# Order of masks and scores on TensorE: rounds 3 and 4 of the row maxima as a joined pair

## The reference, cut to what matters

```
scores = einsum('bhqd,bhkd->bhqk', q, k)
rel    = einsum('bhqd,ld->bhql', q + u, pos)
scores = (scores + rel_shift(rel)) * HEAD_DIM ** -0.5
scores = where(k > q, NEG, scores)
p      = softmax(scores)
ctx    = einsum('bhqk,bhkd->bhqd', p, v)
```

## Time and profile before

| | us |
|---|---|
| median of 3 runs | 2402.88 |
| lowest and highest | 2401.92, 2403.40 |
| the profiled execution's own time | 2404.88 |
| its span, first to last instruction | 2403.1 |
| PE (TensorE matmul) busy | 2285.8 (95%) |
| PEld (weight loads, beside PE) busy | 1976.7 (82%) |
| DVE (VectorE) busy | 2023.2 (84%) |
| ACT (ScalarE) busy | 1837.5 (76%) |
| POOL (GpSimd) busy | 1146.4 (48%) |

### The profile page before, as it was taken

One profiled execution on the slowest core, in us unless ns is written; L12 is line 12 of the kernel. 1 busy time (PEld: TensorE's weight loads), 2 busy tenths in 40 slices (PEclk: granted clock), 3 DMA queues, 4 the chain that ended last, 5 costly groups with the idle time before them and its releaser, 6 DMA issues. The chain is left out here.

```text
span 2403.1 us, 83241 instructions
## 1 busy us (share of the span) xinstructions
PE 2285.8 (95%) x31360; PEld 1976.7 (82%) x31360; DVE 2023.2 (84%) x5071; ACT 1837.5 (76%) x2869; POOL 1146.4 (48%) x2089
## 2 busy tenths in 40 slices
PE   3899999999999999999999999999999999799998
PEld 3688888888888888888888888888888888677776
DVE  6789999888888888888888888888888886677774
ACT  2578888888888888888888888888878888655554
POOL 4355555554555555555454555555445553333332
PEclk8799999999999999999999999999999999899999
DMA  5543333333333333333333333333333331000000
GB/s 130 117 105 97 88 86 91 91 86 92 88 86 91 95 91 92 92 92 85 92 91 93 86 89 91 91 92 91 88 102 88 90 92 51 21 27 27 27 23 19
DMA packets 221161, 196.05 MB, mean 82 GB/s; under 512 B 28897, under 2 KB 217441, under 8 KB 220769
## 3 DMA queue, kind: packets, MB, share of 16 engines
q1 hardware_dynamic: 220768, 190.73, 29.8%
HBM read 14.46 MB, written 4.19 MB: 8 GB/s over the span
## 5 line engine op out<-in xcount | busy, mean ns | idle before, releaser
L1012 DVE TENSOR_REDUCE rowmax<-bank 128x4 f32<-128x1024 f32 (+1 forms) x768 | 914.2, 1218 | 103.3 <-PE bank L580 74.9
L817 ACT ACTIVATE probs<-bank 128x1024 f32<-128x1024 f32 x768 | 738.2, 1024 | 79.4 <-PE bank L640 78.8
L580 PE MATMUL bank<-kstack,qstack 62*128 62x256 f32 (+1 forms) x4096 | 417.9, 301 | 9.5 <-DMA qstack<-base 9.5
L640 PE MATMUL bank<-qstack,kstack 64*128 64x128 f32 (+1 forms) x4096 | 424.3, 300 | 0.0
L858 ACT ACT_TABLE_LOAD x256 | 328.4, 1283 | 4.5
L580 PEld LDWEIGHTS bank<-kstack,qstack 62*128 62x128 f32 x4096 | 317.4, 193 | 9.9 <-issue 9.9
L640 PEld LDWEIGHTS bank<-qstack,kstack 64*128 64x128 f32 x4096 | 317.1, 192 | 0.0
L602 PE MATMUL bank<-maskT_half,pick_half 64*128 64x128 bf16 (+1 forms) x3072 | 267.9, 241 | 24.5 <-DVE rowmax L1012 10.9
L542 PE MATMUL bank<-mask_half,pick_half 64*128 64x128 bf16 (+1 forms) x3072 | 268.8, 243 | 7.9 <-DVE h_all L1047 3.1
L725 PE MATMUL bank<-w,hidden 128*128 128x128 f32 x2048 | 272.6, 277 | 3.1 <-ACT hidden L867 3.1
L660 PE MATMUL bank<-probs,v_pad 128*32 128x256 f32 x4096 | 271.4, 382 | 0.6 <-DVE v_tok L993 0.6
(11 more groups left out here) (154 smaller groups left out, 5259.7 us busy)
## 6 DMA issues: line engine op xcount, KB each, us to landing
qstack<-base SPq DMA_DIRECT2D x768, 128.0 KB, 2.5
kstack<-base SPq DMA_DIRECT2D x384, 128.0 KB, 2.5
turn_x<-turn_c SPq DMA_DIRECT2D x512, 32.0 KB, 1.8
qstack<-maxrows SPq DMA_DIRECT2D x256, 16.0 KB
out<-ot SPq DMA_DIRECT2D x16, 256.0 KB, 2.4
xin<-in_x SPq DMA_DIRECT2D x14, 256.0 KB, 3.1
w<-in_w SPq DMA_DIRECT2D x4, 256.0 KB, 3.2
w_in<-in_w_in SPq DMA_DIRECT2D x1, 768.0 KB, 4.3
```

Source lines behind the costliest of these rows:

```text
L580: last = pe.matmul(bank[:, b0 + b, i * wide:(i + 1) * wide], qstack[rows, r, p0 + i, t * 128:(t + 1) * 128], kstack[rows, r, p0 + i, 0:wid ...
L640: last = pe.matmul(bank[:, b0 + b, i * wide:(i + 1) * wide], kstack[rows, r, p0 + i, kt * 128:(kt + 1) * 128], qstack[rows, r, p0 + i, q0: ...
L817: act.activation(probs[:, k], bank[:, A_BANK[k]:A_BANK[k] + 2, :], ACT.Exp, scale=SCALE).then_inc(exp_done[k], 1)
L1012: dve.tensor_reduce(rowmax[:, n % 2, t, :, p0:p0 + heads], bank[:, M_BANK[k]:M_BANK[k] + 2, :].rearrange("p b (h c) -> p b h c", h=heads), ...
```

## The change

On TensorE's list, the masks of M round 4 are moved ahead of the scores of M round 3. The wait of those masks (for exp_done[4]) moves with them. The number of instructions stays what it is, and the lists of all other engines are unchanged.

```
                 if live(s - 2):
                     m_masks(s - 2, 3)
                 if live(s - 2):
+                    m_masks(s - 2, 4)
+                if live(s - 2):
                     m_scores(s - 2, 3)
-                if live(s - 2):
-                    m_masks(s - 2, 4)
                 if live(s - 2):
                     m_scores(s - 2, 4)
                 if live(s):
```

## The result

Over 17 runs each, the changed kernel has a median of 2409.15 us (2406.41 to 2415.17) and the kernel before 2403.40 us (2400.83 to 2409.18). The forecast was +3.7 us, or 2406.6; the time lies in the range of 2401.5 to 2411.0. Two executions far off, one of e5 (4113.94 us) and one of the kernel before in the batch of e9 to e11 (6417.93 us), count in no ratio. The line of 0.2% that was to part "no change" from "slower" runs through the interval, so by that line alone the result can't be placed; that it is slower is clear.

A forecast was written before the change was run, and what follows sets the result against it. PE is busiest, but DVE's max round 1 releases f2 in each 15.33 us slot; after the change ACT's exponential gates it, 0.03 us later. Over 124 slots, 3.7 us on 2402.88 gives 2406.6, range 2401.5 to 2411.0.

The forecast's parts named there:

- line of 0.2%: Total time: a change under some 0.2%, 4.8 us or 0.039 us per slot, counts as no change, given 0.67.
- f2 is held by DVE: PE's query and key products (f2) start when DVE's max round 1 releases them; PE has about 0.12 us slack per slot.
- The join: Masks, then scores, of rounds 3 and 4 grouped on PE: 0.07 us less per slot, worth nothing alone in front of f2.
- The moved wait: Masks of round 4 on PE wait earlier for ACT's round 4 exponential and stall 0.2 us per slot.
- f2 0.02 to 0.04 later per slot: PE's query and key products load later after the stalled masks and joined scores; 0.03 us taken, over 124 slots 3.7 us.
- DVE's late round 4: DVE's max round 4 starts 0.14 us later; idle time before v_out covers it, with some 0.1 us left.
- Rival A: Round 4's masks restart slowly after the stall: 0.03 us more, 0.06 per slot, 7.4 us, 2410.3; chance 0.20.
- B: The join's gain reaches f2: each slot 0.07 us shorter, 8.7 us faster, 2394.2; chance 0.06.
- C: The stall before f2 is swallowed whole: f2 stays bound by DVE, time stays at 2402.9; chance 0.12.
- Rival D: PE drains fully before f2's load, at the score block's end: 0.10 us per slot, 12.4 us, 2415.3; chance 0.02.

The follow-up runs named there:

- e5: Changed kernel with DVE's max round 1 cut in two, f2 waiting for the first half only; 2408.29 us, ratio 1.0019 to the kernel before.
- e9: Kernel before, with the masks of round 4 placed between the two heads of the scores of round 3; ratio 1.0002.
- e11: Kernel before, with masks of round 4 between the two heads of round 3's scores and DVE's max round 1 cut in two; 2396.68 us, ratio 0.9967.
- e4: Kernel before, old order, with DVE's max round 1 cut in two and f2 waiting for the first half only; 2394.97 us, ratio 0.9970.
- e6: Changed kernel with DVE's max round 1 cut in two and ACT's round 4 exponential on half its columns; 2387.98 us, ratio 0.9939 to the kernel before.
- e7: Kernel before, old order, with DVE's max round 1 cut in two and ACT's round 4 exponential on half its columns; 2391.49 us, ratio 0.9951.
- e2: Changed kernel with ACT's round 4 exponential on half its columns from the second item on; ratio 1.0007 to the kernel before.
- e3: Kernel before, old order, with ACT's round 4 exponential on half its columns from the second item on; ratio 1.0006.
- e1: Kernel before, old order of blocks, with only the wait for exp_done[4] moved ahead of the scores of round 3; 2419.81 us, ratio 1.0075.

## Why the prediction was right

Point by point, by its own steps:

- *f2 is held by DVE, with 0.12 us of slack on PE.* Right. e4 took the hold away and the period fell by 0.11.
- *The join is worth 0.07 us and lies in front of a gate, so nothing.* Right on both counts: e6 against e7 shows the 0.07, e2 against e3 the nothing.
- *The moved wait stalls masks 4 by 0.2 us, until 0.05 or 0.06 after ACT's round 4.* Right: 0.20 us, 0.05 after it, 123 times.
- *f2 0.02 to 0.04 later per slot, 0.03 taken.* Right in size. Of the last 95 gaps between f2's starts, six in either trace are long ones (15.9 to 18.8 us); the mean of the other 89 is 15.324 before and 15.357 after, 0.033 us more. In the slots of the start, with DVE's further work, the gaps go from 15.66 and 16.07 to about 15.70 and 16.12. 124 x 0.033 = 4.1 us lies inside the measured 3.4 to 7.2. (The first ten gaps, 9.7 to 19.9 us, are no such slots; without them it is 3.9.) The forecast's 3.7 is 1.6 below the middle of the interval; whether that rest is more than spread can't be said.
- *DVE's late round 4 is covered.* Right: 0.13 us of cover are left where 0.1 was given.
- *Rival A, masks that restart slowly.* Not so: the load at 1019.32 and the first matmul of those masks start together, as in the earlier trace rows, and their loads are closer together than in flow (e1, above). The matmuls:

```profile
1019.32 0.28 PE L542 MATMUL bank<-mask_half,pick_half 64*128 64x128 bf16 x4
```

- *Rivals B and C, the gain reaches f2, or the stall is swallowed.* Not so: the period neither fell by 0.07 nor stayed; it rose by 0.033.
- *Rival D, a full drain in front of f2.* Not so. The Trainium skill (TensorEngine Tiling (Array Packing), Key Properties) says that a change of tiling mode drains the engine; here f2's first matmul starts at 1035.43, and the scores in front of it end at 1034.78 + 0.72 = 1035.50, so the measurement goes against a drain to the last modelled end.

What the prediction had right is the mechanism and its size. Its favoured outcome, a change within 0.2%, is not borne out: the interval reaches from 0.14% to 0.30%. The weak place was the line at 0.2%: a mechanism sized to 3.7 us beside a line at 4.8 us can't carry 0.67 for "no change" on its own strength, and the measured middle fell just beyond it. Of the 0.27 given to slower, 0.20 was put on rival A and 0.05 on the forecast's own spread; the latter should have had most of it.

The span of the one profiled execution rose by 2.6 us only (2403.1 to 2405.7), since one of the six long gaps was 1.5 us shorter in the trace after (17.30 against 18.78). For a change of this size the mean of the undisturbed slots tells more than two spans.

## What to carry to other kernels

Before steps are joined to save an engine time, look which semaphore opens the step behind them: time saved in front of a gate held by another engine is not seen, and a wait moved forward past work can take the gate over. Compare the due time of the moved wait with its releaser's end in one slot of the timeline; here a stall of 0.2 us stood against 0.12 us of slack and 0.07 us of gain. The gate of the step also points at the better change: cutting the releaser's instruction so that the part which is waited for comes first gave 7 to 10 us, where the join lost 5.

## What was not expected of the hardware

Cutting a reduction of 128x1024 into two of 128x512 costs DVE 0.07 us in all (0.68 us each, started 0.60 apart, 1.28 against 1.21), since the second starts before the first has ended; the bank that is read first is free 0.53 us sooner than the whole would be. And a wait of 0.2 us in front of a joined block left no trace in the granted clock, 1.00 in the long middle stretch as in the earlier trace rows:

```profile
986.00:1479.00 493.00, 488.94 (x7360) 427.90 (x7356) 434.46 (x960) 413.00 (x640) 251.40 (x485) 1.00 0.34 90
```
